# A graph network on one core: moving an edge sort from its own stage into the third gather pass

## The reference: what is computed

```
edge_index = jnp.stack([src, dst])
x = _layernorm(x + _L0_gnn_ref(x, edge_weight1, src, dst, L0_gnn_W, L0_gnn_b), axis=-1)
x = _layernorm(x + _L1_gnn_ref(x, edge_attr_16, dst, src, L1_gnn_W, L1_gnn_W_edge, L1_gnn_a, L1_gnn_ln_scale, L1_gnn_ln_bias), axis=-1)
x = _layernorm(x + _L2_gnn_ref(x, L2_gnn_weight, src, dst, edge_type_16), axis=-1)
x = _layernorm(x + _L3_gnn_ref(x, edge_index, L3_gnn_W, L3_gnn_a), axis=-1)
```

## Time and profile before

| what | us |
|---|---|
| median of three runs | 19102.6 |
| the profiled execution, its own time | 19103.92 |
| its span, first to last instruction | 19101.2 |
| edge stage, first instruction to the next stage's first | 4428.1 to 5469.9 |
| third pass, first gather to the end of the last | 10601.8 to 14649.5 |
| POOL busy over the span | 12531.0 (66%) |
| DVE busy over the span | 9230.2 (48%) |

### The profile page before, as it was taken

One profiled execution on the slowest core, in us unless ns is written; L12 is line 12 of the kernel. 1 busy time (PEld: TensorE's weight loads), 2 busy tenths in 40 slices (PEclk: granted clock), 3 DMA queues, 4 the chain that ended last, 5 costly groups with the idle time before them and its releaser, 6 DMA issues. The chain is left out here.

```text
span 19101.2 us, 250826 instructions
## 1 busy us (share of the span) xinstructions
PE 8282.0 (43%) x37230; PEld 7312.8 (38%) x37231; DVE 9230.2 (48%) x26702; ACT 4224.7 (22%) x18246; POOL 12531.0 (66%) x13216
## 2 busy tenths in 40 slices
PE   2333333336025555555527433333333344444443
PEld 2333333335015555555522333333333344444443
DVE  4333333338957777777752333333333544444444
ACT  1222222221002222222211000000000344444443
POOL 7777777760017777777740677777775677777775
PEclk9999999999999999999999999999999755555555
DMA  1111111111023333333322111111110222222222
GB/s 47 26 26 26 26 26 26 26 29 63 15 64 86 85 85 85 85 85 84 85 69 90 46 26 26 26 26 26 26 26 18 55 53 53 53 53 53 53 53 46
DMA packets 713373, 937.18 MB, mean 49 GB/s; under 512 B 303241, under 2 KB 324509, under 8 KB 710871
## 3 DMA queue, kind: packets, MB, share of 16 engines
q0 software_dynamic: 423856, 454.56, 11.9%
q1 hardware_dynamic: 289448, 481.91, 7.9%
HBM read 723.02 MB, written 206.21 MB: 49 GB/s over the span
## 5 line engine op out<-in xcount | busy, mean ns | idle before, releaser
L416 POOL DMA_INDIRECT l_rows<-t_d,l_idx_st x3232 | 3063.1, 948 | 1705.1 <-issue 920.3
L475 DVE TENSOR_TENSOR acc<-acc,l_ps 128x65 f32 (+1 forms) x6464 | 1439.4, 223 | 5258.4 <-DVE acc L475 3592.4
L1042 POOL DMA_INDIRECT gat_rows<-t_d,gat_idx_st x3232 | 3067.9, 949 | 1007.9 <-issue 933.2
L416 POOL DMA_INDIRECT l_rows<-in_x,l_idx_st x3232 | 3065.2, 948 | 994.6 <-issue 984.3
L1714 POOL DMA_INDIRECT p_rows<-x_d,p_idx_st x3232 | 3063.4, 948 | 993.2 <-issue 956.3
L431 PE MATMUL l_ps<-l_rows,l_oh 128*128 128x64 f32 x6464 | 1482.9, 424 | 2586.1 <-DVE acc L475 1680.0
L431 PE MATMUL l_ps<-l_msg,l_oh 128*128 128x65 f32 x6464 | 1482.7, 421 | 2579.3 <-DVE acc L475 2319.1
L431 PEld LDWEIGHTS l_ps<-l_rows,l_oh 128*128 128x128 f32 x6464 | 1409.1, 330 | 2661.2 <-DVE acc L475 2586.6
L431 PEld LDWEIGHTS l_ps<-l_msg,l_oh 128*128 128x128 f32 x6464 | 1408.7, 330 | 2653.2 <-DVE acc L475 2589.3
L1146 PE MATMUL gat_ps<-gat_msg,gat_oh 128*128 128x72 f32 x6464 | 1488.4, 425 | 1059.7 <-DVE gat_msg L1206 1059.7
L1146 PEld LDWEIGHTS gat_ps<-gat_msg,gat_oh 128*128 128x128 f32 x6464 | 1409.1, 330 | 1176.3 <-DVE gat_tot L1226 1143.1
(11 more groups left out here) (289 smaller groups left out, 11806.4 us busy)
## 6 DMA issues: line engine op xcount, KB each, us to landing
cur_d<-gat_cur SPq DMA_DIRECT2D x404, 288.0 KB
gat_keyrow<-keyb_d SPq DMA_DIRECT2D x404, 256.0 KB
p_keyrow<-keyb_d SPq DMA_DIRECT2D x404, 256.0 KB, 3.2
l_rows<-in_x,l_idx_st POOLq DMA_INDIRECT x3232, 2.4
gat_rows<-t_d,gat_idx_st POOLq DMA_INDIRECT x3232
l_rows<-t_d,l_idx_st POOLq DMA_INDIRECT x3232, 2.4
p_rows<-x_d,p_idx_st POOLq DMA_INDIRECT x3232
t_d<-t_tab SPq DMA_DIRECT2D x98, 512.0 KB, 2.6
```

What stands on the lines that cost most here:

```text
L416: pool.indirect_dma_start(rows[:, r, s, :], None, table, bass.IndirectOffsetOnAxis(idx_st[:, r, s:s + 1], 0)).then_inc(s_rows[r], 16)
L475: dve.tensor_tensor(there, there, part, ALU.add).then_inc(s_acc, 1)
L1042: pool.indirect_dma_start(rows[:, r, s, :], None, m.t1_d, bass.IndirectOffsetOnAxis(idx_st[:, r, s:s + 1], 0)).then_inc(s_rows[r], 16)
```

## The change

The sort leaves the edge stage, which keeps the edge scores alone; the copy of the scores to `es_se` moves from ACT to DVE. The third pass gets a function of its own, `second_pass`. On DVE its first 224 groups are written out as straight-line code instead of a loop, and behind the additions of each of them stands one step of the sort (`sort()`, a generator; `yield` ends what goes into one group). The exchange reads both halves from SBUF, as before, with the operands in the other order. The sort's setup (the first three portions), each step of the network, and the two last conversions are one portion each; a quarter exchange has two empty portions ahead of its wait for the DMAs. The additions take the form of the fourth pass: eight window numbers in one load. SP loads `src` and `dst` behind the pass's own tables and issues the quarter DMAs and the two results from there. The barrier at the pass's end also waits for the sorted arrays.

```
-def edge_scores_and_sort(nc, m, edge_attr, W, We, a, src, dst):
+def edge_scores(nc, m, edge_attr, W, We, a):
...
                 act.copy(eaT[:, b], pt[:, b, :, 0:EP]).then_inc(s_eaT, 1)
-                act.wait_ge(s_mm, n + 1)
-                alone(act)
-                act.copy(se[:, bass.ds(n * CH, CH), :],
-                         po[0:EP, b, 0:CH * E8 * HEADS].rearrange("p (c k) -> p c k", c=CH)).then_inc(s_se, 1)
...
+            with dve.Fori(0, N // 2) as i:
+                for b in range(2):
+                    n = i * 2 + b
+                    dve.wait_ge(s_mm, n + 1)
+                    alone(dve)
+                    dve.tensor_copy(se[:, bass.ds(n * CH, CH), :],
+                                    po[0:EP, b, 0:CH * E8 * HEADS].rearrange("p (c k) -> p c k", c=CH)).then_inc(s_se, 1)
...
+def second_pass(nc, m, table, idx_d, src, dst):
...
+        SORTING = RINGS * (-(-(sum(3 if kind == "quarters" else 1 for kind, _, _ in network()) + 6) // RINGS))
...
+        def loop(eng, body, beside):
+
+            for n in range(SORTING):
+                body(n, n % RINGS)
+                next(beside, None)
+            with eng.Fori(SORTING // RINGS, TURNS - 1) as i:
+                for r in range(RINGS):
+                    body(i * RINGS + r, r)
+            for r in range(RINGS):
+                body((TURNS - 1) * RINGS + r, r)
...
         def _(sp):
...
+            sp.dma_start(idx[:], idx_d).then_inc(s_tab, 16)
+            sp.dma_start(key[:], m.key_d).then_inc(s_tab, 16)
             sp.dma_start(ka[:, 0:EPR], src.rearrange("(p f) -> p f", p=P)).then_inc(s_keys, 16)
             sp.dma_start(kb[:, 0:EPR], dst.rearrange("(p f) -> p f", p=P)).then_inc(s_keys, 16)
...
+            def add(n, r):
+                _, js = nc.values_load_multi_w_load_instructions(m.winrow[0:1, bass.ds(n * U, U)], [mybir.EngineType.DVE],
+                                                                 min_val=0, max_val=WINS - 1)
+                dve.wait_ge(s_mm, n + 1)
+                for s, j in enumerate(js):
+                    there = m.acc[:, bass.ds(j, 1), 0:D].rearrange("p o w -> p (o w)")
+                    if since(n, 1) or s > 0:
+                        dve.wait_ge(s_acc, n * U + s)
+                    dve.tensor_tensor(there, there, ps[:, r % 2, s, 0:D], ALU.add).then_inc(s_acc, 1)
+
+            def body(n, r):
+                dve.wait_ge(s_staged, n + 1)
+                if since(n, 2):
+                    dve.wait_ge(s_mm, n - 1)
+                onehots(dve, m, oh[:, r % 2], key_st[:, r], s_oh)
+                if since(n, 1):
+                    add(n - 1, (r - 1) % RINGS)
...
+                for kind, j, k in network():
+                    if kind == "exchange":
+                        x, y = pairs_of(keys[0], j, k), pairs_of(keys[1], j, k)
+                        if k is None:
+                            h = x[:, :, 1]
+                            dve.tensor_tensor(y[:, :, 0], h, x[:, :, 0], ALU.min)
+                            so(dve.tensor_tensor(y[:, :, 1], h, x[:, :, 0], ALU.max))
...
+                    else:
+                        yield
+                        yield
+                        swaps += 1
+                        x, y, s = keys[0], keys[1], low[:, j:j + 1]
+                        dve.wait_ge(s_swap, 64 * swaps)
...
-            edge_scores_and_sort(nc, m, edge_attr, W1, W1e, a1, src, dst)
+            edge_scores(nc, m, edge_attr, W1, W1e, a1)
...
-                sum_pass(nc, m, "l2", m.t2_d.rearrange("j p (r o) -> (j p r) o", o=D), m.rel_d, False)
+                second_pass(nc, m, m.t2_d.rearrange("j p (r o) -> (j p r) o", o=D), m.rel_d, src, dst)
```

More of the change, by code:

```diff
@@ L724, in _ @@
[L724 to L758, removed]
@@ new lines, with network @@
+PADKEY = 8589934080.0
+FBITS = 12
+COLS = 1 << FBITS
+SLOTS = P * COLS
+def network():
+    for k in range(1, FBITS):
+        for j in reversed(range(k)):
+            yield "exchange", j, k
+    for k in range(FBITS, FBITS + 8):
+        yield "sides", k - FBITS, None
+        for b in (6, 5):
+            if b < k - FBITS:
+                yield "quarters", b, None
+        if k > FBITS:
+            yield "lanes", None, None
+            for b in reversed(range(min(5, k - FBITS))):
+                yield "exchange", b, None
+            yield "lanes", None, None
+        for j in reversed(range(FBITS)):
+            yield "exchange", j, None
@@ L806, in _, with stage @@
+            sp.wait_ge(s_sort, links + 2)
+            sp.dma_start(m.by_src_d.rearrange("(p f) -> p f", p=P), y[:]).then_inc(s_sorted, 16)
             sp.dma_start(m.to_dst_d.rearrange("(p f) -> p f", p=P), kb[:]).then_inc(s_sorted, 16)
-            sp.wait_ge(s_out, 16)
             sp.wait_ge(s_sorted, 32)
+        @block.scalar
+        def _(act):
+            def stage(n, r):
+                if since(n, RINGS):
+                    act.wait_ge(s_rows[r], rows_in(n, r) - 16 * U)
+                    act.wait_ge(s_oh, n - RINGS + 1)
+                    alone(act)
+                act.copy(idx_st[:, r, :], idx[:, bass.ds(n * U, U)])
+                act.copy(key_st[:, r, :], key[:, bass.ds(n * U, U)]).then_inc(s_staged, 1)
+            def body(n, r):
+                if not (isinstance(n, int) and n + 2 >= GROUPS):
+                    stage(n + 2, (r + 2) % RINGS)
+            act.wait_ge(s_tab, 32)
+            stage(0, 0)
+            stage(1, 1)
+            for n in range(RINGS):
+                body(n, n)
+            with act.Fori(1, TURNS - 1) as i:
+                for r in range(RINGS):
+                    body(i * RINGS + r, r)
+            for r in range(RINGS):
+                body((TURNS - 1) * RINGS + r, r)
@@ new lines, in _, with body @@
+        @block.gpsimd
+        def _(pool):
+            def body(n, r, first, last):
+                pool.wait_ge(s_staged, n + 1)
+                if not first:
+                    pool.wait_ge(s_mm, n - RINGS + 1)
+                alone(pool)
+                for s in range(U):
+                    pool.indirect_dma_start(rows[:, r, s, :], None, table,
+                                            bass.IndirectOffsetOnAxis(idx_st[:, r, s:s + 1], 0)).then_inc(s_rows[r], 16)
+            turns(pool, body)
@@ new lines, in _, with body @@
+        @block.tensor
+        def _(pe):
+            def body(n, r, first, last):
+                pe.wait_ge(s_oh, n + 1)
+                pe.wait_ge(s_rows[r], rows_in(n, r))
+                if after(first, 2, r):
+                    pe.wait_ge(s_acc, (n - 1) * U)
+                for s in range(U):
+                    ins = pe.matmul(ps[:, r % 2, s, 0:D], oh[:, r % 2, s, :], rows[:, r, s, :], start=True, stop=True)
+                ins.then_inc(s_mm, 1)
+            turns(pe, body)
+        @block.vector
```

166 lines of the change are left out of this document (101 added, 65 removed).

## The result

The changed kernel takes 18868.9 us (median of 4 runs, 18867.4 to 18871.8), the kernel before 19100.4 (19095.3 to 19102.9): a ratio of 0.9879, 95% interval 0.9862 to 0.9896. It is 231 us faster. The prediction was 504 us faster, 18599, with a range that ended at 18850. The profiled execution has a span of 18869.2 us against 19101.2 before.

What follows compares the result with a forecast made beforehand. DVE's sort bounds the edge stage and POOL's gathers the third pass, where DVE becomes the bound for 224 groups. 19103.9 - 663 + 181 - 24 + 2 = 18599.9, median 18599 us; range 18530 to 18850.

Steps and rivals of the forecast that it cites:

- Edge stage, -662 to -663: Edge stage: with the sort gone it ends at 4807.5 instead of 5469.9 us, once the last scores have left.
- POOL's pace of 10.02 us: Third pass: gathers of 1.2524 us each set the pace, 10.02 us for a group of eight.
- DVE's cost of a group, 6.47 us without the step: Third pass: DVE's serial one-hots, load, additions and waits per group; with a 4.5 us exchange 10.97 us, over POOL's 10.02.
- the 0.13 for instruction blocks: Third pass: fetching written-out code in 81 blocks at 0.35 us each adds 0.13 us to DVE's group.
- Run-ahead over the one-hots: Third pass: DVE's window-number load starts 0.45 us after the first one-hot, not 1.4, because the list runs past queued instructions.
- The sum without the lock: Whole kernel: 18599 us, with DVE the bound for 224 groups of the third pass (+181 us); 65% chance.
- The lock: Third pass: exchanges with two SBUF inputs hold up POOL's gathers; a rival at 9%, not priced in the forecast.
- that rival, +976 us: Third pass: all the sort's 976 us is added to POOL's time, 19418 us; two thirds of 9% was for slower.
- One-input steps: Third pass: 17 sort steps of 2.35 us may hold gathers, 40 us at most, but POOL's spare time makes it nothing.
- Lead, -24: Third pass: POOL gets three groups ahead while DVE is the bound, and the last 180 groups start from that lead.
- the small terms: Third pass: keys landing behind the tables delay first groups by 5 us, last additions are 3 us shorter: +2.
- the partial lock: Third pass: exchanges block gathers for part of their time, ending at 18850 to 19060 us; the rest of the lock's 9%.

Runs made afterwards that it cites:

- e1: Changed kernel, but ScalarE copies the exchange's upper half to PSUM and both exchange instructions read that operand there: 18496.0 us, ratio 0.9684.
- e7: Kernel before, with the second pass's one-hot instruction (L1176) taking its row operand from SBUF instead of PSUM: 19397.4 us, ratio 1.0134.
- e8: e1 plus one extra DVE instruction per group behind the sort, form changing every 24 groups (five forms and a copy): 18692.4 us, one run.
- e4: Changed kernel with the edits of e1 and e3 together (operand in PSUM, steps in three of four groups): 18481.2 us, ratio 0.9677.
- e3: Changed kernel with sort steps in three of four groups, some 300 groups instead of 224, both operands in SBUF: 18860.9 us, ratio 0.9874.
- e2: Changed kernel with only the exchange's first instruction (minimum) taking an operand from PSUM, the maximum reading both from SBUF: 18752.4 us, ratio 0.9816.

## Why the prediction was wrong, point by point

- **Edge stage, -662 to -663: right.** Measured 664.0, of which 2.5 arose ahead of the stage, so 661.5 in it. Its first transposes start 9.8 us into the stage instead of 17.3 (7.5 sooner, forecast 7); from the issue of the scores' DMA to the next stage's first copy are 49.3 us (forecast 48.0); the score copy has its slack.
- **POOL's pace of 10.02 us, once nothing disturbs it: right.** The 180 last groups have it.
- **DVE's cost of a group, 6.47 us without the step: too high by 0.7.** In e1's unwaited group it is 3.07 (first one-hot to first addition; forecast 0.45 + 3.05) + 2.68 (11505.33 to 11508.01; forecast 2.55 + 0.14) + 0.04 (11512.49 to 11512.53; forecast 0.15) = 5.79, and this group has no trace of the 0.13 for instruction blocks, though these came nearly as counted: the page's queue of instruction loads has 125 packets where the earlier trace rows has 52, 73 more (forecast 81).

```profile
q14 instruction: 125, 1.02, 0.0%
```

- **Run-ahead over the one-hots: right, and complete.** Forecast that the load starts 0.45 us behind the first one-hot; it starts with it, and runs under all eight. The rows of one group (kernel after, durations min/median/max ns, first and last start):

```profile
L867 DVEq TENSOR_LOAD <-winrow x1: 597/597/597, 10110.8 to 10110.8; - x1
```

```profile
L309 DVE TENSOR_SCALAR l_oh<-row,l_key_st x8: 277/277/349, 10110.8 to 10112.2; 128x128 f32<-128x128 f32 x8
```

  Eight instructions can stand between the running list and the engine. The Trainium skill (Advanced Engine Details and Errata, Engine Queue Depths) gives VectorE a depth of 8; the trace agrees.
- **The sum without the lock: the right kind, 103 us too high.** e1 is that kernel: 18496 instead of 18599. Its first 224 groups go from 9943.9 to 12242.2, 10.26 us each, and cost 224 x 0.24 = 54 us where I had 181. With 5.79 my own sum would have been 224 x 5.79 + 976 = 2273 us against 2244, +29; what the other 25 are, no run separates.
- **The lock, priced at nothing: the step that failed.** It costs 373 us (18869 - 18496), by keeping POOL the bound at 11.97 us per group where the prediction had DVE the bound at about 10.8. The prediction named the mechanism as a rival and then gave it 9%, on one row: the earlier trace rows. The row was misread. I called L1176 an instruction "with both inputs in SBUF"; the kernel's code says that one of them is in PSUM (see e7), and the trace's row names only `own` and `key_st` and not the memory. e7 measured what the row would have looked like if the sentence had been true. So the case had, before the run, no evidence against the rule of the Trainium skill (SBUF — State Buffer, Who interferes with whom), that a DVE instruction with two SBUF inputs contends with a GpSimd instruction that reads SBUF. The trace agrees with it: gathers of 0.94 us take 2.14 and 1.90. e1, e7 and e8 show that it is the operand's memory that decides.
- **The size of that rival, +976 us if all of it blocks: too high.** The sort's 976 us cost POOL 435 (3497.8 against 3063.1 us busy for the 3232 gathers, pages of the two kernels). Of an exchange's 4.5 us some 2 are paid, because a gather already past its held point goes on under it. "A blocked gather would be over 2 us long" was right, and it was.
- **One-input steps, "17 x 2.35 = 40 us at most, nothing": wrong in the reason.** They hold gathers too (e8: 1.9 us each), and POOL has no room of its own in a group; what hid them in the forecast was a DVE-bound pass. In e4, POOL-bound, they and the three L959 make most of the 41 us that are left.
- **Lead, -24, and the small terms:** the lead rests on POOL being early, which it never was here (13 us of waiting for PE in 2600). So it fell away.
- **The range** ended at 18850, 19 us short. It left the partial lock (18850 to 19060) out as a case of 3%. The result lies in it. That the range was missed by so little is no merit: without the lock the kernel takes 18496, below the range's lower end of 18530, so a forecast with DVE's group rightly priced and no lock would have been further off.

In one line: -664 as forecast; the pass +159 forecast, -104 for a cheaper DVE group and all that hangs on it, +377 for the lock (profiled spans, 18869.2 - 18492.6), makes +432. The -104 is read from e1, where DVE is the bound; in the changed kernel itself POOL is.

## What to carry to other kernels

Before work is moved on VectorE beside gathers that GpSimd issues, list each instruction with the memory of every input and its rate: two inputs in SBUF, or one at the doubled rate, held the gathers in the experiments here (on f32); one input in PSUM made the same work free for them, even when an idle ScalarE had to copy it there (2 us per step, and 373 us gained). Such instructions cost by their count and by how they fall on the gathers, not by their share of busy time, and spreading them out did not help (e3). And when one row is to overrule a rule, look up in the code what the row's operands are; the row's names alone do not say it.

## What the hardware showed beyond that

- The hold goes nearly one way. Exchanges take 2.28 us with or without a gather beside them; only instructions at the doubled rate were sometimes longer, 2580 ns at most instead of 2346, and a copy 2440 instead of 2285.
- There are two points at which a gather can be held. An instruction with two SBUF inputs caught only gathers that started under it, and they ended 0.8 us after it. The edge is sharp: in e2, gathers that started up to 0.03 us after the start of such an instruction (L937) took 0.94 or 0.95 us, and those from 0.04 us on were held, the first of them 3.06 us long. An instruction at the doubled rate also caught one under way, which ended 0.12 us after it; in e8 it caught those that had started up to 0.47 us before it, and none of the three that had started 0.48 us or more before. The Trainium skill (SBUF — State Buffer, A bandwidth-pool intuition that's wrong (but worth ruling out)) has the second as the writing of descriptors, blocked until the end of the instruction and some 115 ns more; e8's 0.12 us agrees with it. That the first is the reading of the gather's indices fits, but no run here tells it apart from another read.
- A hold can pass from one instruction to the next. The longest gather of the changed kernel, 7.48 us from 9988.33 on, lies under the four instructions of the sort's first exchange (each some 2.0 us, the last ends at 9994.99) and ends 0.82 us after the last of them.
- A 128x4096 transpose of 4.44 us, one input at the single rate, held nothing: in e4 three gathers ran beside it at 0.94 us.

```profile
11515.31 4.44 DVE L950 STREAM_TRANSPOSE l_kc<-l_ka 128x4096 f32<-128x4096 f32 x1
11516.17 0.94 POOL L872 DMA_INDIRECT l_rows<-t_d,l_idx_st  x1 [0.30 <-issue]
11517.41 0.94 POOL L872 DMA_INDIRECT l_rows<-t_d,l_idx_st  x1 [0.30 <-issue]
11518.66 0.94 POOL L872 DMA_INDIRECT l_rows<-t_d,l_idx_st  x1 [0.30 <-issue]
```

Left open: whether the doubled-rate steps and the three L959, given to ScalarE or sent through PSUM as well, would bring e4 down to POOL's 18440 us. It wasn't tried.
